# Score tiles, key and query projections and the rest of a block's TensorE work spread over its 18 slots in a cross-attention and mixture-of-experts kernel

## What is computed

```python
x, lat = layer_norm(ctx), layer_norm(layernorm(x))
q = lat @ Wq;  k, v = split(concat([x, lat]) @ Wkv)
attn = softmax(q @ k.T * 64 ** -0.5);  x = x + (attn @ v) @ Wout
x = x + ffn(layernorm(x))       # shared network + 32 experts, 4 of them for each token
```

## Time and profile before

| | us |
|---|---|
| median of 3 runs | 1649.9 (1648.56 to 1650.05) |
| the profiled execution | 1647.04 |
| its span, first to last instruction | 1645.3 |
| TensorE busy | 1513.9 (92%) |
| VectorE, GpSimd, ScalarE busy | 1050.6, 940.0, 796.0 |

### The profile page before, as it was taken

The page is one execution under the profiler, slowest core; times in us unless marked ns, Lnnn a source line. Parts: engine busy times, 40 slices in busy tenths (PEclk is TensorE's granted clock), DMA queues, the critical chain, the costliest instruction groups (busy, mean ns, idle before and its releaser), DMA issues.

```text
span 1645.3 us, 23810 instructions
## 1 busy us (share of the span) xinstructions
PE 1513.9 (92%) x8086; PEld 1067.2 (65%) x8086; DVE 1050.6 (64%) x1574; ACT 796.0 (48%) x1501; POOL 940.0 (57%) x751
## 2 busy tenths in 40 slices
PE   3899999999999999999999999988899999999995
PEld 2565555555655555565565555546779999999995
DVE  7556666576565665767767776556656566666662
ACT  3355444544444445544454344533336566666662
POOL 4457766666566765766667777784343343334333
PEclk8899999999999999999999999998899999999998
DMA  3032440000000000000011000101246666667664
GB/s 99 16 80 70 101 91 11 24 15 10 18 8 22 15 10 24 15 11 15 10 28 31 27 28 27 44 30 58 81 161 167 175 191 180 172 177 193 171 173 89
DMA packets 99282, 117.93 MB, mean 72 GB/s; under 512 B 10595, under 2 KB 78181, under 8 KB 99173
## 3 DMA queue, kind: packets, MB, share of 16 engines
q1 hardware_dynamic: 82149, 96.97, 20.1%
q0 software_dynamic: 17056, 19.97, 6.2%
HBM read 74.93 MB, written 35.06 MB: 67 GB/s over the span
## 4 chain that ended last, share of the span: by engine, by line
PE 72%; DVE 15%; ACT 6%; POOL 3%; issue 2%; DMA 1%; ACTq 0%; SPq 0%; DVEq 0%; POOLq 0%
PE ps_o L947 13%; PE ps_t L804 8%; PE ps_m L909 8%; PE ps_m L804 8%; PE ps_st L804 7%; PE ps_st L932 6%; DVE arena_r L1307 5%; PE ps_st L936 5%; ACT arena L1590 3%; PE ps_m L841 3%; PE ps_o L841 3%; PE ps_t L967 2%; DVE arena L1318 2%; PE ps_t L1014 2%; PE ps_t L954 2%
## 5 line engine op out<-in xcount | busy, mean ns | idle before, releaser
L744 POOL TENSOR_TENSOR arena<-arena 128x512 f32<-128x512 f32 (+1 forms) x512 | 660.3, 1292 | 345.9 <-ACT arena L1590 307.3
L1590 ACT ACTIVATE arena<-ps_st 128x512 f32<-128x512 f32 (+1 forms) x576 | 327.3, 596 | 463.2 <-PE ps_st L936 430.3
L1307 DVE TENSOR_REDUCE arena_r<-ps_m 128x1 fp32r<-128x1107 f32 x256 | 334.2, 1306 | 179.4 <-PE ps_m L909 175.4
L779 POOL DMA_INDIRECT acc_rows<-arena,ids x96 | 150.8, 1571 | 267.1 <-ACT arena L1653 239.5
L932 PE MATMUL ps_st<-arena_r 128*128 128x512 f32 (+1 forms) x576 | 247.9, 430 | 27.9 <-ACT arena L1590 27.8
L947 PE MATMUL ps_o<-arena 128*64 128x512 f32 (+1 forms) x1152 | 268.5, 601 | 0.0
L936 PE MATMUL ps_st<-arena_r 68*128 68x512 f32 (+2 forms) x576 | 229.7, 399 | 1.9 <-DVE arena_r L1314 1.9
L909 PE MATMUL ps_m<-arena_r 128*128 128x370 f32 x768 | 194.7, 362 | 31.0 <-DVE arena_r L1307 23.1
L909 PEld LDWEIGHTS ps_m<-arena_r 128*128 128x128 f32 x768 | 130.1, 192 | 118.3 <-DVE arena_r L1307 65.6
L932 PEld LDWEIGHTS ps_st<-arena_r 128*128 128x128 f32 (+1 forms) x576 | 106.9, 186 | 106.7 <-ACT arena L1590 84.2
L947 PEld LDWEIGHTS ps_o<-arena 128*64 128x64 f32 (+1 forms) x1152 | 74.2, 137 | 143.2 <-issue 132.0
(11 more groups left out here) (211 smaller groups left out, 1870.9 us busy)
## 6 DMA issues: line engine op xcount, KB each, us to landing
arena<-in_L_ffn_wg_dram SPq DMA_DIRECT2D x32, 512.0 KB, 4.6
arena<-in_L_ffn_wu_dram SPq DMA_DIRECT2D x32, 512.0 KB, 6.4
arena<-in_L_ffn_wd_dram SPq DMA_DIRECT2D x32, 512.0 KB, 3.9
x_slots<-route SPq DMA_DIRECT2D x5, 2176.0 KB, 12.9
arena<-x_slots SPq DMA_DIRECT2D x32, 272.0 KB, 2.7
arena_r<-arena_r SPq DMA_DIRECT2D x30, 275.2 KB, 3.7
arena<-in_L_xattn_Wkv_dram SPq DMA_DIRECT2D x32, 128.0 KB, 2.4
arena<-x_slots SPq DMA_DIRECT2D x32, 68.0 KB, 2.4
```

Of the source, the lines that this page charges most:

```text
L744: pool.tensor_tensor(total, probsT[0:rows, h, 0, :] if kt == 1 else total, probsT[0:rows, h, kt, :], ALU.add).then_inc(added, 1)
L779: pool.indirect_dma_start(out=dst[:, :], in_=y_sb[par][:, c, 0:w], in_offset=None, compute_op=ALU.add, out_offset=bass.IndirectOffsetOnAxi ...
L1307: dve.tensor_reduce(neg[h][:, c:c + 1], ps_m[:, :, 0:PIECE_W], AX.XY, ALU.max, negate=True)\
L1590: act.activation(probsT[0:rows, h, kt, :], ps_st[0:rows, n % 2, :], ACT.Exp).then_inc(exp_done, 1)
```

## The change

Within a block the steps are hung behind other slots. The same steps are done, none is added or left out. In even blocks the second maximum goes from slot (0,0) to (0,1), the last three av steps of the block before from (0,5) to (0,4) and (0,7), the second step of q's high parts and its low part from around (0,5) to (0,3). In odd blocks the k pieces go from (0,0), (0,2), (0,3) to (0,0), (0,2), (0,4), with their maxima behind the next slot, and q goes from (0,5), ahead of three av steps, to (0,6), behind them. In both, sum goes from (0,8) to the next slot (1,0), and the second half of out goes from (1,6) to (0,2) of the following block.

```diff
--- before.py
+++ after.py
@@ -80,27 +80,36 @@
         last_values = values(old, prev, (6, 7, 8))
         own_max = [own("max", d, 1, i) for i in range(4)]
         next_max = [nxt("max", n, 0, i) for i in range(4)]
-        out = [old("out", prev, i) for i in range(2)]
-        after = {(0, 8): [own("row", d, 1), old("sum", prev)],
+        out_a = old("out", prev, 0)
+        out_b = ("out", (d - 2) % QUADS, 1), int(d < 2)
+        after = {(0, 1): [own_max[1]],
+                 (0, 8): [own("row", d, 1)],
+                 (1, 0): [old("sum", prev)],
                  (1, 1): [],
                  (1, 2): [old("norm", prev), next_max[0]],
-                 (1, 3): first_values + [next_max[1]]}
+                 (1, 3): first_values + [next_max[1]],
+                 (1, 4): [out_a, next_max[2]]}
         if project:
-            after[0, 0] = [own_max[0]] + project_k(0) + [own_max[1], k_low[0]]
-            after[0, 2] = project_k(2) + [own_max[2], k_low[2]]
-            after[0, 3] = project_k(1) + [k_low[1]]
-            after[0, 5] = project_q() + [q_again] + last_values + [q_low, own_max[3]]
-            after[1, 4] = [out[0], next_max[2]]
+            after[0, 0] = [own_max[0]] + project_k(0)
+            after[0, 1] += [k_low[0]]
+            after[0, 2] = project_k(2) + [out_b]
+            after[0, 3] = [own_max[2], k_low[2]]
+            after[0, 4] = project_k(1)
+            after[0, 5] = [own_max[3], k_low[1]] + last_values
+            after[0, 6] = project_q() + [q_again, q_low]
             after[1, 5] = [nxt("v", pp, 0), next_max[3]]
-            after[1, 6] = more_values + [nxt("row", n, 0), out[1]]
+            after[1, 6] = more_values + [nxt("row", n, 0)]
             after[1, 7] = [nxt("v", pp, 1)]
             after[1, 8] = [nxt("v", pp, 2)]
         else:
-            after[0, 0] = [own_max[0]] + project_q() + [own_max[1]]
-            after[0, 3] = [own_max[2]]
-            after[0, 5] = [q_again] + last_values + [q_low, own_max[3]]
-            after[1, 4] = [out[0], next_max[2]]
-            after[1, 6] = [out[1], next_max[3]] + more_values + [nxt("row", n, 0)]
+            after[0, 0] = [own_max[0]] + project_q()
+            after[0, 2] = [out_b]
+            after[0, 3] = [q_again, q_low, own_max[2]]
+            after[0, 4] = last_values[:2]
+            after[0, 5] = [own_max[3]]
+            after[0, 7] = last_values[2:]
+            after[1, 6] = [next_max[3]]
+            after[1, 7] = more_values + [nxt("row", n, 0)]
         if d == 0:
             after[1, 1] = [own("w", 1)] + after[1, 1]
         if d == 2:
@@ -123,7 +132,7 @@
         put(block, 1, 3, "mid", *events)
 
     def b(block, *events):
-        put(block, 1, 6, "row", *events)
+        put(block, 1, 7 - block % 2, "row", *events)
 
     def c(block, *events):
         put(block, 0, 5, "end", *events)
@@ -135,7 +144,7 @@
         put(block, 1, 0, "end", *events)
 
     def ring_early(block, *events):
-        put(block, 0, 2, "end", *events)
+        put(block, 0, 3, "end", *events)
 
     for j in range(FILLS):
         put(1 + j, 0, 6, "end", ("fill", j))
@@ -224,15 +233,14 @@
             for n, (ev, back) in enumerate(slot):
                 place = "row" if ev[0] == "row" else "mid" if n == len(slot) - 1 else None
                 plan += [(new, T) for at, new in more if at == place]
-                late = (ev, T - back) == (("out", LAST_D - 1, 1), LAST_T)
-                if 0 <= T - back < TURNS and not late:
+                if 0 <= T - back < TURNS:
                     plan.append((ev, T - back))
                     if (ev, T - back) == (("out", LAST_D - 1, 0), LAST_T):
                         plan.append((("out", LAST_D - 1, 1), LAST_T))
-                elif T == 0 and ev[0] == "out":
+                elif T == 0 and ev[0] == "out" and ev[1] == LAST_D:
                     plan.append((("cen", ev[2]), 0))
             plan += [(new, T) for at, new in more if at == "end"]
-    end = [ev for slot in slots for ev, back in slot if back == 1]
+    end = [ev for slot in slots for ev, back in slot if back == 1 and ev != ("out", LAST_D - 1, 1)]
     assert [ev[0] for ev in end] == ["av"] * 3 + ["sum", "norm", "out", "out"]
     scats = [[("scat", g, i) for i in range(SCATTERS)] for g in range(GROUPS)]
 
```

## The result

| | before | after |
|---|---|---|
| median, us | 1650.0 (1648.6 to 1651.3, 4 runs) | 1812.1 (1805.0 to 1817.0, 4 runs) |
| ratio to before, 95% interval | | 1.098 (1.095 to 1.101) |
| the profiled execution | 1647.0 | 1815.8 |
| its span, mean granted clock of TensorE | 1645.3, 0.978 | 1814.1, 0.939 |

The change costs 162 us. The forecast was 1768, 118 more than before, in a range of 1712 to 1812: the sign and the three waits are as forecast, the loss is 44 us larger, and the time came out at the very end of the range.

A forecast was written before the change was run, and what follows sets the result against it. TensorE, busy 92% of the span, was taken as the bound. Odd blocks 75, even blocks 24, rest 5 and clock 15 gave 119 on 1647.0, 1766; with the median 2.9 above, the forecast was 1768, range 1712 to 1812.

The forecast's parts named there:

- The three waits of odd blocks: TensorE waits 1.9 us before out's half, 1.6 before k piece 1, 3.3 around the second head's first tile.
- Even blocks: New waits of 3.7 us less 2.2 gained: 1.5 us longer in each of 16 blocks, 24 us.
- (a): Even blocks, slot 3: q's copies and low part precede the third maximum's reduction, so the fourth maximum waits 1.4 us.
- (b): Even blocks, row: with sum gone from behind it, 0.6 us of the wait for the mask result is uncovered.
- (c): Even blocks, behind sum: VectorE's reciprocal, weights' split and reduction make the second maximum wait 0.8 us.
- (d): Even blocks: without out's half between the third and fourth maxima, VectorE cannot keep their spacing, 0.7 us lost.
- Rest: Routing transposes behind q's bank in slot 3 and a longer weights' split in later turns: +5 us, from 0 to 10.
- The clock: Half rate behind the 3.3 us wait costs 1.5 us in 10 of 15 odd blocks: 15 us, bounds 0 and 27.
- The rival that had half rate behind all three waits: Odd blocks: each new wait brings half rate, 15 x 3 x 1.6 us on top of 104, total 1826; chance 0.10.
- Absorbed waits: Waits already there take up new ones; even blocks come out even, odd ones lose only 3.5 us: 1702; chance 0.15.
- TensorE late enough: TensorE reaches the waiting steps late, so new waits are mostly covered: 1594; chance 0.05, shared with another case.
- The gain: Fewer empty-slot and small waits: 2.0 to 2.3 us per even block, 1.5 per odd, about 56 us if nothing new waits.

The follow-up runs named there:

- The kernel with three edits: Changed kernel with out's second half back at (1,6), odd blocks' q back ahead of av, even blocks' third maximum ahead of q's copies: 1648.8 us.
- the kernel without the new waits: Changed kernel with q ahead of av, row at (0,7), out's half not between k pieces, third maximum ahead of q's copies, weights' split late: 1613.3 us.

## Why the prediction came out as it did

**The three waits of odd blocks** (1.9, 1.6 and 3.3): right in place, releaser and size (1.95, 1.14, 1.95 + 1.01 in the block shown). The walk put the mask's matmul 22.4 us behind the block's first tile; with the clock held up it stands at 697.66 - 674.8 = 22.9. Waits and gains together are 5.8 a block instead of 5.0, 12 us over 15 blocks; about 0.5 of it is the walk's to that matmul, and 0.3 is gain that did not come in the second head: from there to the next block's first tile the old times less the 0.5 give 18.5 (631.68 to 650.4 before, plus sum's 1.0, less out's 0.7), and the trace has 716.5 - 697.66 = 18.8.

**Even blocks** (+1.5): +1.6 measured; (a), (b) and (c) each have a row and an experiment of their own, though (c) gave 8 us and not 13 when it was taken away. (d) has a row, 0.55. The kernel with three edits shows that the match is better than the terms deserve: there 1.1 us an even block are missing.

**Rest** (+5) can't be told apart; it lies within the waits' total, 113 against 104.

**The clock** (15 us, bounds 0 and 27): here the forecast failed. It is 50, beyond its upper bound. It was put together as 10 stretches of 3.5 us at a cost of 0.43 each us. Measured are 28 stretches in 15 odd blocks, 5.4 us each in the mean (150 us), at a cost of 0.33.

The number of stretches is what was most wrong. The forecast let only the 3.3 us wait count, since a wait of 2.4 us in the earlier trace rows had full rate behind it. But 1.95 us ahead of out's half was followed by half rate in 13 of 15 odd blocks, each time before the next wait began. That one row was a single draw. In the kernel without the new waits and with sum back at (0,8), the same job waits 2.28 us for the same norm, and has half rate behind it (timeline and a window of that kernel, of the length of the one in the earlier trace rows):

```profile
1071.69 3.47 PE L971 MATMUL ps_t<-wout_sb,arena 128*128 128x256 f32 x8 [2.28 <-POOL arena L753]
...
1071.50:1074.50 3.00, 2.81 (x7) 2.28 (x8) 0.69 (x1) 0.00 (x0) 2.67 (x4) 0.50 0.13 46
```

So one window behind one wait says nothing: a wait of 2 us may or may not bring the low rate. Half rate followed out's wait of 1.95 us in 13 of 15 odd blocks of the changed kernel, in 10 with the third maximum moved, and in 9 with q ahead or with the second head's wait filled. What decides it no run here shows.

The length comes second. The first stretch lasts 6.9 us in the block shown, and k piece 1's wait lies inside it; five more blocks are like that, and in the seven whose first stretch ends before that wait it is half as long. Whether the wait prolongs it was not tested apart. Last, half rate costs a third of its length and not nearly half, at least in part because TensorE's waits take some of it up: k piece 1 waits 1.46 and 1.47 us in the two blocks without a first stretch, and 1.07 to 1.14 in the block shown and six others.

The rule of the Trainium skill, TensorE: Matmul & The Clock Gate, "HAM oscillation", weighed there, says that a loop with a long idle gap in every round falls to half rate every round. The changed kernel's trace bears it out better than the row that was set against it: every odd block did, though the same first two waits in the kernel with q ahead did so in 9 of 15. The 24 us worked out from it had the same short stretch, once a block. The rival that had half rate behind all three waits, 1826, is the nearer of the two in its mechanism: two stretches a block, not three. The forecast's own spread, 1740 to 1795, had taken the clock at no more than its bound and missed the result; the range ended at 1812, where the result came out, only because 1826 had been given one chance in ten. That it came out so near is luck. (The sum as it stands gives 1769, not 1768.)

**The rivals.** Absorbed waits, 1702: no, odd blocks lost more than the walk, not less. TensorE late enough, 1594: no, its own waits are in the trace of every odd block.

**The gain** (56 us if nothing new waits): the kernel without the waits has 36 of it, and 40 with sum left where it was.

## What to carry to other kernels

A slot with no work of its own on the busiest engine is not free room. Before a step is moved there, list what stands ahead of it in the line for its bank and in the in-order queue of each engine that serves it, and count the busiest engine's work between the producer's issue and its user; here sum and q were each the cover of a chain on VectorE or ScalarE (0.6 and 3.3 us) that lay open when they left, and out's half came to stand in front of a bank that such a chain had not yet freed (1.9). Price a wait on TensorE with the clock behind it: where the blocks had run at full rate, new waits that cost a net 113 us cost another 50 by the lower rate they brought. Don't take one wait that went without as a rule: count how often waits of that length had half rate behind them, in as many places as the traces have. Where such a wait can't be taken away, matmuls whose result nobody reads can hold the clock.

## What the runs showed of the hardware

360 added matmuls (up to 24 in an odd block), whose results are never read, made the kernel 50 us faster, 1812.1 to 1762.6, with every step left in its place. A wait of 1.95 us of TensorE was followed by a granted clock of 0.50 in 13 of 15 odd blocks of one kernel, in 10 of another and in 9 of two more; waits of 1.95 and 1.01 us with a single matmul between were in 15 of 15 of the changed kernel and in 13 of 15 with out's half moved back. A wait of 2.4 us had 1.00 behind it in the kernel before, one of 2.28 at the same job had 0.50 in another. At the lower rate six matmuls of 512 columns took 2.93 us instead of 1.66.
